# An attention and mixture-of-experts layer whose first stage works in rounded three-part products, with its stores, first score passes, row scatter and last stores rearranged

## The chip, the cores and the metric

The kernel runs on one core of one Trainium2 chip. The metric is the device time of one execution in microseconds (us); "before" is the kernel as it stood, "after" the changed one.

## The reference

One transformer layer on 4096 tokens of width 256. The tokens are normalised, the same `xn` goes through 16-head attention and through a feed-forward part with eight routed experts (two for each token) and one shared expert, and all three are added.

```python
xn = _layernorm(x, axis=-1)                  # x: (1, 4096, 256)
q, k, v = xn @ Wq.T, xn @ Wk.T, xn @ Wv.T    # 16 heads of 16
attn = softmax(einsum('bqhd,bkhd->bhqk', q, k) / sqrt(256))
out  = einsum('bhqk,bkhd->bqhd', attn, v)
scores = softmax(xn @ gate_w.T); idx = top_k(scores + gate_b, 2)
expert(x) = silu((x @ w1 + b1) * (x @ w3 + b3)) @ w2 + b2      # 256 -> 352 -> 256
result = x + out + sum_k scores[idx_k] * expert_idx_k(xn) + shared_expert(xn)
```

## The kernel before

The work is written out by hand for each engine; semaphores order it, and each engine takes its instructions in the order of the code.

**First stage.** The tokens come in eight chunks of 512 (`NCH`). VectorE normalises them (`variances`, `deviations`, `normalise`), TensorE transposes a chunk (`turn_xn`), ScalarE copies it to SBUF (`take_xn`), and `project` makes four blocks (two of queries, two of keys) of 128 rows by 512 tokens, each out of two full-precision matmuls. ScalarE writes a rounded copy of each block (`split`) and its square, VectorE the rest that the rounding left (`residual`), and SyncE stores both to DRAM (`qk_parts`), from where heads are later loaded. `norms` sums the squares; from them a bound on the scores is worked out, which head 0 needs as a shift for each query (`spart`, stored to `qshift_parts`). After the chunks `value_rows` makes the values and the router's inputs in 16 pairs of token tiles, ScalarE copies each pair (`keep_values`), and only then do the scores begin.

**Heads.** A head has 128 groups of scores (`GH`). For each group TensorE does two matmuls of 50 rows (`scores`), ScalarE one exponential of 1024 columns (`probs`), and for each two groups TensorE does four matmuls of values. The semaphore `s_scores` counts groups and is the clock of the other queues. Heads 0 and 15 are plain (`plain_head`). In heads 1 to 14 the feed-forward units are woven in, four for a head (`mixed_head`): unit u does `up_both(u, 0..2)` and the two `down_tile`s of unit u-1, and has 32 groups of scores. Units 0 to 7 are the shared expert on the first tokens (`shared`, `SA = 8`), units 8 to 46 are routed.

**How a unit gets its tokens.** GpSimd loads the tokens of a shared unit from `xnT_rows` (`load_shared`), VectorE splits them in a rounded part and a rest at the end of the unit before (`tokens_hi`, `tokens_lo`), and TensorE waits for this (`s_xboth`) before `up_both(u, 0)`. GpSimd's other work at that time is `scatter`: sixteen times it loads 256 rows of x, normalises them and writes them to their experts' slots with four indirect transfers. Both stand in one queue, in this order:

```python
            scatter(0)
            scatter(1)
            for u in range(SZ + 1):
                if u + 2 < SA or u + 2 in (SZ, SZ + 1):
                    load_shared(u + 2)
                for v in range(2 + 3 * u, min(5 + 3 * u, SH)):
                    scatter(v)
```

So `load_shared(6)` stands behind scatters 0 to 13. The first scatter waits for all 128 groups of head 0. Unit 8 on the SyncE side (`load_slots(8)`) waits for all scatters.

**End.** SyncE stores the last 16 columns of the result when the last head's sum is done.

## Time and profile before

| | us |
|---|---|
| three runs, median (lowest to highest) | 2173.07 (2171.87 to 2174.39) |
| the profiled execution | 2174.21 |
| its span (first to last instruction) | 2172.3 |
| TensorE busy in the span | 2152.4 |
| ScalarE busy | 2009.4 |
| VectorE busy | 800.5 |
| GpSimd busy | 246.0 |

The profiled execution lasted 1.9 us longer than its span. A busy TensorE is not TensorE at its peak: matmuls overlap in the records, so what one costs is read from the distance between starts.

### The profile page before, as it was taken

To read this page: it belongs to the slowest core of one execution; us is meant where nothing else is said; L and a number is where in the kernel's file an instruction comes from. 1 tells how busy PE (TensorE), PEld (TensorE's weight loads), DVE (VectorE), ACT (ScalarE), POOL (GpSimd) and SP (SyncE) were. 2 spreads that over 40 slices of the span, in tenths; PEclk is the share of its full clock that TensorE was granted. 3 is DMA by queue.
4 is the path that set the end of the run, shared out by engine and by line. 5 is a ranking of instruction groups with operands and counts; after the bars stand their busy time and mean duration, and the time that the engine had idled before them with its cause. 6 is when DMAs were issued, how large, how long until landed. Compare 5 with 4: busy or idle time off the path is not lost.

```text
span 2172.3 us, 37982 instructions
## 1 busy us (share of the span) xinstructions
PE 2152.4 (99%) x15638; PEld 965.2 (44%) x15638; DVE 800.5 (37%) x1515; ACT 2009.4 (93%) x2209; POOL 246.0 (11%) x242
## 2 busy tenths in 40 slices
PE   9999999999999999999999999999999999999998
PEld 4632344444444444444444444444444444444322
DVE  6321143344344334334334434334334334544200
ACT  4599999999999999999999999999999999999998
POOL 0100465610000000000000000000000002223200
PEclk9999999999999999999999999999999999999999
DMA  7671334332222222213132222213213222332120
GB/s 254 206 280 33 91 121 130 100 90 66 63 78 63 76 57 79 78 54 85 48 77 70 77 64 69 78 50 83 75 50 90 63 69 75 105 97 66 57 78 3
DMA packets 223595, 187.24 MB, mean 86 GB/s; under 512 B 112039, under 2 KB 194558, under 8 KB 223166
## 3 DMA queue, kind: packets, MB, share of 16 engines
q1 hardware_dynamic: 211598, 149.41, 24.3%
q0 software_dynamic: 11824, 35.40, 5.0%
q8 instruction: 123, 2.02, 0.4%
q14 instruction: 50, 0.41, 0.1%
HBM read 130.21 MB, written 54.53 MB: 85 GB/s over the span
## 4 chain that ended last, share of the span: by engine, by line
PE 92%; ACT 7%; DVE 1%; DMA 0%; issue 0%; DVEq 0%
PE PS L672 41%; PE PS L659 29%; PE PS L684 12%; ACT probs L866 6%; PE PS L695 6%; PE PS L565 2%; PE PS L602 1%; PE PS L575 0%; DVE stats L972 0%; PE PS L554 0%; DMA resid<-in_x 0%; DVE probs L996 0%; ACT probs L818 0%; DVE o_t L1169 0%; DVE mv L975 0%
## 5 line engine op out<-in xcount | busy, mean ns | idle before, releaser
L866 ACT ACTIVATE probs<-PS 128x1024 f32<-128x1024 f32 x2048 | 1920.0, 1080 | 96.0 <-PE PS L659 81.8
L672 PE MATMUL PS<-probs,v_head 128*32 128x512 f32 x8192 | 1002.8, 601 | 1.1 <-ACT probs L866 0.8
L659 PE MATMUL PS<-q_ring,k_stack 50*128 50x512 f32 x4096 | 741.3, 446 | 7.0 <-ACT probs L866 6.2
L659 PEld LDWEIGHTS PS<-q_ring,k_stack 50*128 50x128 f32 x4096 | 332.6, 185 | 627.2 <-ACT probs L866 569.6
L672 PEld LDWEIGHTS PS<-probs,v_head 128*32 128x32 f32 x8192 | 206.6, 108 | 448.2 <-issue 359.6
L1194 DVE TENSOR_SCALAR gate_in<-PS,bias_sb 128x256 f32<-128x256 f32 x165 | 79.6, 482 | 754.9 <-PE PS L684 739.5
L684 PE MATMUL PS<-x_hi,w_hi 128*128 128x256 f32 (+1 forms) x660 | 201.3, 305 | 0.0
L684 PE MATMUL PS<-x_hi,w_lo 128*128 128x256 f32 (+1 forms) x660 | 186.5, 283 | 0.0
L684 PE MATMUL PS<-x_lo,w_hi 128*128 128x256 f32 (+1 forms) x660 | 185.6, 281 | 0.0
L921 POOL DMA_DIRECT2D slot_y<-y_sb x39 | 27.9, 716 | 1285.1 <-DVE y_sb L1262 1251.6
L684 PEld LDWEIGHTS PS<-x_hi,w_hi 128*128 128x128 f32 (+1 forms) x660 | 118.6, 180 | 60.0 <-issue 60.0
L684 PEld LDWEIGHTS PS<-x_lo,w_hi 128*128 128x128 f32 (+1 forms) x660 | 118.5, 180 | 0.0
L684 PEld LDWEIGHTS PS<-x_hi,w_lo 128*128 128x128 f32 (+1 forms) x660 | 118.4, 179 | 0.0
L695 PE MATMUL PS<-w_hi,hid_hi 128*128 128x256 f32 x330 | 99.0, 300 | 0.0
L1262 DVE COPY y_sb<-PS 128x512 f32<-128x512 f32 x39 | 27.0, 692 | 188.6 <-PE PS L695 188.6
L695 PE MATMUL PS<-w_lo,hid_hi 128*128 128x256 f32 x330 | 93.3, 283 | 0.0
L695 PE MATMUL PS<-w_hi,hid_lo 128*128 128x256 f32 x330 | 93.1, 282 | 0.0
L1223 DVE TENSOR_TENSOR w_lo<-w_raw,w_hi 128x1408 fp32r<-128x1408 f32 x55 | 89.7, 1630 | 1.9
L1199 DVE SCALAR_TENSOR_TENSOR prod<-PS,bias_sb,gate_in 128x256 f32<-128x256 f32 x165 | 79.7, 483 | 5.9
L1169 DVE STREAM_TRANSPOSE o_t<-PS 128x512 f32<-128x512 f32 x32 | 22.9, 717 | 154.3 <-PE PS L672 154.2
L914 POOL DMA_INDIRECT slot_x<-y_sb,pos x64 | 70.2, 1097 | 19.1 <-issue 14.3
L695 PEld LDWEIGHTS PS<-w_hi,hid_hi 128*128 128x128 f32 x330 | 62.8, 190 | 13.3 <-issue 13.3
(137 smaller groups left out, 1098.2 us busy)
## 6 DMA issues: line engine op xcount, KB each, us to landing
w_raw<-in_w SPq DMA_DIRECT2D x110, 352.0 KB
k_stack<-qk_parts SPq DMA_DIRECT2D x120, 128.0 KB
w_raw<-in_w SPq DMA_DIRECT2D x55, 256.0 KB
q_ring<-qk_parts SPq DMA_DIRECT2D x384, 32.0 KB
slot_x<-part_a SPq DMA_DIRECT2D x39, 256.0 KB, 2.3
slot_in<-slot_x SPq DMA_DIRECT2D x156, 64.0 KB, 2.4
slot_y<-y_sb POOLq DMA_DIRECT2D x39, 256.0 KB, 2.5
k_stack<-qk_parts SPq DMA_DIRECT2D x136, 64.0 KB
```

The costliest lines, as they stand in the source:

```text
L565: last = pe.matmul(bank(2 + j), wqk[:, j // DT, dt, (j % DT) * P:(j % DT + 1) * P], cols, start=(dt == 0), stop=(dt == DT - 1))
L659: last = pe.matmul(bank(2 * score_buffer(turn, g) + r), k_stack[rows, kt * P:(kt + 1) * P], q_ring[rows, sweep, i * QC:(i + 1) * QC], star ...
L672: last = pe.matmul(bank(O_BANK)[VW * j:VW * (j + 1), :], v_head[:, kt, :], probs[:, slot, (j % 2) * QC:(j % 2 + 1) * QC], start=(kt == 0), ...
L684: last = pe.matmul(f_half(w)[0:FT[j], :], a[u % 2][:, w, dt, j * P:j * P + FT[j]], b[:, dt * CH:(dt + 1) * CH], start=(n == 0), stop=(n == ...
L695: last = pe.matmul(f_half(t), a[0:rows, j, t * P:(t + 1) * P], b[0:rows, j, :], start=(n == 0), stop=(n == 8))
L866: nc.scalar.activation(probs[:, prob_slot(g), :], bank(2 * score_buffer(h, g), 2), ACT.Exp, scale=ENERGY_SCALE).then_inc(s_exp, 1)
L914: nc.gpsimd.indirect_dma_start(out=slot_x, out_offset=bass.IndirectOffsetOnAxis(ap=pos[:, u * TPU + t, k:k + 1], axis=0), in_=rows[:, t, : ...
L921: nc.gpsimd.dma_start(slot_y[(u - SA) * CH:(u - SA + 1) * CH, :].rearrange("(t p) d -> p t d", p=P), y_sb[:, u % 2, :].rearrange("p (t d) ...
L1194: V.tensor_scalar(gate_in[0:FT[j], :], f_half(0)[0:FT[j], :], bias_sb[0:FT[j], u % 2, j:j + 1], 0.5, ALU.add, ALU.mult).then_inc(s_gin, 1)
L1199: V.scalar_tensor_tensor(prod[u % 2][0:FT[j], j, :], f_half(1)[0:FT[j], :], bias_sb[0:FT[j], u % 2, 3 + j:4 + j], gate_in[0:FT[j], :], ALU ...
L1223: V.tensor_tensor(w13_lo[u % 2][:, :, :, :], w13_raw[:, :, :, :], w13_hi[u % 2][:, :, :, :].bitcast(f32), ALU.subtract).then_inc(s_w13, 1)
L1262: V.tensor_copy(y_sb[:, u % 2, :], bank(F_BANK)).then_inc(s_yc, 1)
```

## The change

1. **Rounded products.** Chunk 0 is projected as before. For chunks 1 to 7 and all values, tokens and weights are each split in a rounded part and a rest, and each product becomes three rounded matmuls (high by high, low by high, high by low). ScalarE writes two copies of each transposed chunk (`take_tokens`), VectorE makes the rests (`tokens_low`, and once for the weights).
2. **A new order.** Queries are made with the keys for chunks 0 to 3 only; those of chunks 4 to 7 follow after all keys (`late_queries`). The values of pairs 0 to 9 are made between the projections, pairs 10 to 15 at the end. Stores of keys and queries are separate, and each chunk of tokens is stored to `xnT_rows` as it is made, where before all 4 MB went out in one transfer after the first stage.
3. **Buffers.** Query chunks 6 and 7 are kept in what later are probability buffers and in `part_a`. So `keep_values(12)` waits until the store of query chunk 6 has landed, and group 6 of head 0 waits for the shift's second half.
4. **Shift in halves.** The first half, which head 0's first sweep reads, is stored and loaded before the second is there.
5. **Filler.** Between the first score groups of head 0 TensorE repeats a score matmul pair seven times into banks that nobody reads; the first values come one step earlier. The routing counts stand 4 steps later in head 0.
6. **Scatter.** `scatter(u)` waits for group GH + 32 + 8u, where it was GH + 10u.
7. **Last stores.** Two of the last four stores are issued by ScalarE.

```diff
+FIRST = NCH // 2
+XRING = 4
+PAIRS = NT // 2
+SIDE_PAIR = 5
+LATE_PAIR = 10
+LN_GROUPS = ((0, 4), (4, 8), (8, 12), (12, 16), (16, 24), (24, NT))
+LN_LOAD = (0, 1, 2, 2, 3, 4)
 
...
+def key_job(c):
+
+    return 4 * c if c < FIRST else 4 * FIRST + DT * (c - FIRST)
+
+
+def query_job(c):
+
+    return 4 * c + DT if c < FIRST else 4 * FIRST + DT * c
+
...
+            def store_keys(c):
+
+                for s, ready in enumerate((s_hi, s_res)):
+                    sp.wait_ge(ready, key_job(c) + DT)
+                    sp.dma_start(store_v[s][:, DT:2 * DT, c * QC:(c + 1) * QC], key_part[c % 2][:, s, :, :].bitcast(f32)).then_inc(s_kst[c % 2], 16)
...
+                sp.wait_ge(s_xt, DT * (c + 1))
+                sp.dma_start(x_rows[:, :, c * QC:(c + 1) * QC], xfull[:, c % 2, :, :]).then_inc(s_xd[c % 2], 16)
+                store_keys(c)
                 if c:
-                    sp.wait_ge(s_store[part_of(c - 1)], stored(c - 1))
+                    sp.wait_ge(s_kst[(c - 1) % 2], stored(c - 1))
                     load_k_chunk(c - 1)
-                if c == QCH:
-                    load_q_rows(0, 0)
-            sp.wait_ge(s_store[part_of(NCH - 1)], stored(NCH - 1))
+                if c < FIRST:
+                    store_queries(c)
+            for half in range(2):
+                sp.wait_ge(s_qst[half], stored(FIRST - 2 + half))
+            load_q_rows(0, 0)
+            store_queries(4)
+            store_queries(5)
+            sp.wait_ge(s_kst[(NCH - 1) % 2], stored(NCH - 1))
             load_k_chunk(NCH - 1)
-            for s in range(NP_):
-                sp.wait_ge(s_s1, s + 1)
-                sp.dma_start(qshift_parts[s].rearrange("h (c t) -> c h t", c=NCH), spart[:, s, :].bitcast(f32)).then_inc(s_sst, 16)
+            store_shift(0)
+            store_queries(6)
+            store_queries(7)
+            sp.wait_ge(s_sst, 16 * NP_)
...
+            def project(c, w, i, b):
+
+                cols = slice(i * P, (i + 1) * P)
+
+                def moving(buf, dt):
+                    return buf[:, dt, :] if w else buf[:, dt, :].rearrange("p (t j r) -> p j t r", t=TPC, j=QCH)
+
+                hi, lo = xh[c % XRING], xl[c % XRING]
+                for dt in range(DT):
+                    pe.wait_ge(s_xh, DT * c + dt + 1)
+                    pe.matmul(bank(b), wqk_hi[:, w, dt, cols], moving(hi, dt), start=(dt == 0), stop=False)
+                    pe.matmul(bank(b), wqk_lo[:, w, dt, cols], moving(hi, dt), start=False, stop=False)
+                pe.wait_ge(s_xl, c + 1)
+                for dt in range(DT):
+                    last = pe.matmul(bank(b), wqk_hi[:, w, dt, cols], moving(lo, dt), start=False, stop=(dt == DT - 1))
+                last.then_inc(s_qk, 1)
...
+            def value_rows(n):
+
+                if n == 0:
+                    pe.wait_ge(s_vwl, 1)
+                if n < SIDE_PAIR or n == LATE_PAIR:
+                    pe.wait_ge(s_xt, DT * turned[0])
+                    pe.wait_ge(s_xh, DT * turned[0])
+                if n == SIDE_PAIR:
+                    pe.wait_ge(s_res, query_job(FIRST - 1) + DT)
+                if n == LATE_PAIR + 1:
+                    pe.wait_ge(s_res, NCH * NJ)
+                if n == LATE_PAIR + 2:
+                    pe.wait_ge(s_qn, 2)
+                if 0 < n <= LATE_PAIR:
+                    pe.wait_ge(s_vc, n)
+                if n >= LATE_PAIR + 3:
+                    pe.wait_ge(s_vc, n - 2)
+                for i in range(2):
+                    c, t = (2 * n + i) // TPC, (2 * n + i) % TPC
+                    rows = slice(t * P, (t + 1) * P)
                     for dt in range(DT):
+                        dst = bank(pair_bank(n) + i)[:, 0:VE]
+                        pe.matmul(dst, xh[c % XRING][:, dt, rows], wvg_hi[:, dt, :], start=(dt == 0), stop=False)
+                        pe.matmul(dst, xh[c % XRING][:, dt, rows], wvg_lo[:, dt, :], start=False, stop=False)
+                        last = pe.matmul(dst, xl[c % XRING][:, dt, rows], wvg_hi[:, dt, :], start=False, stop=(dt == DT - 1))
+                last.then_inc(s_v, 1)
+                paired[0] = n + 1
 
...
             turn_first()
+            first_project(1, 0)
+            first_project(1, 1)
+            turn_xn(1)
+            first_project(0, 0)
+            first_project(0, 1)
             pe.wait_ge(s_hb, 2)
-            for c in range(NCH):
-                pe.wait_ge(s_xt, c + 1)
-                project(c, 0)
-                project(c, 1)
+            key_norms(0)
+            for c in range(1, FIRST):
+                keys(c, 0)
+                query_norms(c - 1)
+                keys(c, 1)
+                if c > 1:
+                    value_rows(2 * c - 3)
+                queries(c, 0)
+                turn_xn(c + 1)
+                queries(c, 1)
+                key_norms(c)
+                value_rows(2 * c - 2)
+            for c in range(FIRST, NCH):
+                keys(c, 0)
+                if c == FIRST:
+                    query_norms(FIRST - 1)
                 if c < NCH - 1:
                     turn_xn(c + 1)
-                if c:
-                    norms(c - 1)
-                project(c, 2)
-                project(c, 3)
-            norms(NCH - 1)
-
...
+            late_queries(4, 0)
+            late_queries(4, 1)
             pe.wait_ge(s_mk, 1)
             pe.transpose(bank(7)[0:1, 0:P], kmax[:, 0:1], ident_sb[:, :]).then_inc(s_kt, 1)
-            value_rows(1)
+            late_queries(5, 0)
+            query_norms(4)
+            late_queries(5, 1)
             pe.wait_ge(s_krow, 1)
             pe.matmul(bank(7)[:, P:P + 1], krow[0:1, 0:P], ones_sb[0:1, 0:1], start=True, stop=True).then_inc(s_kb, 1)
-            value_rows(2)
-            value_rows(3)
-            value_rows(4)
+            late_queries(6, 0)
+            query_norms(5)
+            late_queries(6, 1)
+            late_queries(7, 0)
+            query_norms(6)
+            late_queries(7, 1)
+            value_rows(10)
+            query_norms(7)
+            value_rows(11)
             pe.wait_ge(s_gcol, 1)
             pe.transpose(bank(6)[0:1, 0:P], qbound[:, 1:2], ident_sb[:, :]).then_inc(s_grow, 1)
-            for n in range(5, NT // 2):
+            for n in range(12, PAIRS):
                 value_rows(n)
...
+                    if h == 0 and k == 1:
+                        continue
                     next_scores(2)
-                    if h == 0 and k == 20:
+                    if h == 0 and k == 24:
...
+            def filler(count):
+
+                for n in range(count):
+                    for r in range(2):
+                        rows = slice(r * HALF, r * HALF + ROWS)
+                        pe.matmul(bank(F_BANK + r), k_stack[rows, 0:P], q_ring[rows, 0, 0:QC], start=True, stop=True)
+
             next_scores(SB)
+            filler(3)
+            next_scores(1)
+            filler(2)
+            next_scores(1)
+            filler(2)
+            next_values(1)
             plain_head(0)
...
+            def take_tokens(c):
 
                 act.wait_ge(s_tr, c + 1)
...
+            def keep_values(n):
+
+                if n == 12:
+                    act.wait_ge(s_qst[0], stored(6))
+                act.wait_ge(s_v, n + 1)
+                src = bank(pair_bank(n), 2).rearrange("p (i n) -> p i n", i=2)
+                nc.scalar.activation(v_all[:, 2 * n:2 * n + 2, :], src[:, :, 0:VE], ACT.Copy).then_inc(s_vc, 1)
 
...
+                    if h == 0 and g == 6:
+                        act.wait_ge(s_sst, 32 * NP_)
...
+            act.wait_ge(s_resid, SH + SWEEPS)
+            for c in range(NCH - 2, NCH):
+                nc.scalar.dma_start(out_v[:, c * TPC:(c + 1) * TPC, D - HD:D], resid[:, c * TPC:(c + 1) * TPC, D - HD:D]).then_inc(s_out, 16)
...
-                pool.wait_ge(s_scores, GH + 10 * u)
+                pool.wait_ge(s_scores, GH + 32 + 8 * u)
...
+            def tokens_low(c):
+
+                for dt in range(DT):
+                    dve.wait_ge(s_xt, DT * c + dt + 1)
+                    dve.wait_ge(s_xh, DT * c + dt + 1)
+                    last = V.tensor_tensor(xl[c % XRING][:, dt, :], xfull[:, c % 2, dt, :], xh[c % XRING][:, dt, :].bitcast(f32), ALU.subtract)
+                last.then_inc(s_xl, 1)```

TensorE's order in the middle of the first stage, of before: chunk 3 and what follows it (`early` holds the transposed tokens, `hones_b` sums the squares).

```order
L554 MATMUL PS<-ident_sb,probs 128x128 x8
L575 MATMUL PS<-probs,hones_b 128x512 x4
L565 MATMUL PS<-early,probs 128x512 x8
L554 MATMUL PS<-ident_sb,probs 128x128 x8
L575 MATMUL PS<-probs,hones_b 128x512 x4
```

The changed kernel on the same engine, in the chunks that make keys only (`x_parts` holds the two parts of the tokens):

```order
L696 MATMUL PS<-probs,hones_b 128x512 x2
L664 MATMUL PS<-x_parts,wqk_hi 128x512
L665 MATMUL PS<-x_parts,wqk_lo 128x512
L664 MATMUL PS<-x_parts,wqk_hi 128x512
L665 MATMUL PS<-x_parts,wqk_lo 128x512
L668 MATMUL PS<-x_parts,wqk_hi 128x512 x2
L640 MATMUL PS<-ident_sb,probs 128x128 x8
```

Two full-precision matmuls of a block have become six rounded ones, and a chunk has two blocks here where it had four.

ScalarE at the end of the first stage, before: the last blocks, the root for the shift, the value pairs, then the exponentials.

```order
L818 ACTIVATE probs<-PS 128x512
L836 ACTIVATE probs<-PS 128x512 [waits s_nr]
L843 ACTIVATE v_all<-PS 128x528 [waits s_v,s_store1]
L843 ACTIVATE v_all<-PS 128x528 [waits s_v]
L848 ACTIVATE kmax<-PS 128x1 [waits s_kb]
L843 ACTIVATE v_all<-PS 128x528 [waits s_v] x14
L866 ACT_TABLE_LOAD
```

And in the changed kernel (L1031 is the rounded copy of a query block, L1040 a value pair):

```order
L1031 ACTIVATE part_a<-PS 128x512 [waits s_qk]
L1032 ACTIVATE probs<-PS 128x512
L1040 ACTIVATE v_all<-PS 128x528 [waits s_v]
L1092 ACTIVATE probs<-PS 64x512 [waits s_nq]
L1040 ACTIVATE v_all<-PS 128x528 [waits s_v]
L1040 ACTIVATE v_all<-PS 128x528 [waits s_v,s_qst0]
L1040 ACTIVATE v_all<-PS 128x528 [waits s_v] x3
L1112 ACT_TABLE_LOAD
```

The query blocks now stand right before the last value pairs, and pair 12 waits for a store (`s_qst0`).

SyncE's queue ahead of the first scores, in the changed kernel, from the stores of query chunk 5 to the load of the shift:

```order
L455 DMA qk_parts<-part_q 128x2x512 [waits s_hi]
L455 DMA qk_parts<-part_q 128x2x512 [waits s_res]
L414 DMA k_stack<-qk_parts 32x1x512 [waits s_kst1]
L416 DMA k_stack<-qk_parts 16x512
L414 DMA k_stack<-qk_parts 32x1x512
L416 DMA k_stack<-qk_parts 16x512
L463 DMA qshift_parts<-probs 4x16x512 [waits s_s1] x2
L455 DMA qk_parts<-probs 128x2x512 [waits s_hi]
L455 DMA qk_parts<-probs 128x2x512 [waits s_res]
L455 DMA qk_parts<-part_a 128x2x512 [waits s_hi]
L455 DMA qk_parts<-part_a 128x2x512 [waits s_res]
L432 DMA q_ring<-qshift_parts 2x4x128 [waits s_sst]
```

Before, all stores of queries stood ahead of the values; now six of the last eight stand among the loads that the first scores need.

## Rows read from the trace of the kernel before

**Rows 1.** The page: the span.
```profile
span 2172.3 us, 37982 instructions
```

**Rows 2.** Stretches: from:to, length; PE, PEld, DVE, ACT, POOL; clock; DMA; GB/s.
```profile
80.00:90.00 10.00, 8.82 (x38) 6.07 (x37) 5.37 (x11) 4.20 (x9) 6.33 (x3) 1.00 0.96 367
...
1220.00:1260.00 40.00, 40.00 (x310) 18.95 (x300) 14.10 (x24) 38.22 (x42) 0.71 (x1) 1.00 0.27 71
```

**Rows 3.** Chain that ended last, first stage: start us, us, what.
```profile
61.75 6.87 PE PS L565 x16
...
70.35 6.87 PE PS L565 x16
...
93.36 19.60 PE PS L602 x88
```

**Rows 4.** Timeline, first stage, ScalarE and VectorE: start us, us, instruction.
```profile
78.41 0.59 ACT L818 ACTIVATE probs<-PS 128x512 bf16<-128x512 f32 x1
...
78.89 0.60 ACT L817 ACTIVATE part_a<-PS 128x512 fp32r<-128x512 f32 x1
...
23.38 1.28 DVE L1009 TENSOR_TENSOR v_all<-PS,v_all 128x512 fp32r<-128x512 f32 x2
```

**Rows 5.** Timeline of TensorE: rounded products in a unit; chain: two score groups.
```profile
434.59 0.28 PE L684 MATMUL PS<-x_lo,w_hi 128*128 128x256 f32 x1
...
434.71 0.28 PE L684 MATMUL PS<-x_hi,w_lo 128*128 128x256 f32 x1
...
163.29 0.84 PE PS L659 x4
```

**Rows 6.** Timeline and busy time by stretch: the start of head 0.
```profile
113.64 0.96 PE L659 MATMUL PS<-q_ring,k_stack 50*128 50x512 f32 x6 [0.70 <-ACT v_all L843]
...
114.90 4.69 ACT L866 ACTIVATE probs<-PS 128x1024 f32<-128x1024 f32 x5
...
124.55 16.59 ACT L866 ACTIVATE probs<-PS 128x1024 f32<-128x1024 f32 x18
...
116.00:120.00 4.00, 3.59 (x14) 1.14 (x16) 0.00 (x0) 3.58 (x4) 0.00 (x0) 0.57 0.97 414
```

**Rows 7.** Timeline: SyncE's store of a chunk; GpSimd's wait for the last one.
```profile
69.53 3.02 SPq L400 DMA_DIRECT2D qk_parts<-part_a  x2
...
93.39 0.31 POOL L885 MEMSET w_raw<- 32x256 f32 x1 [6.94 <-DMA qk_parts<-part_a]
```

**Rows 8.** Timeline of GpSimd: scatters 0 and 1, loads of units 5, 6.
```profile
234.03 0.72 POOL L904 DMA_DIRECT2D y_sb<-in_x  x1 [111.10 <-PE PS L659]
...
244.86 0.79 POOL L904 DMA_DIRECT2D y_sb<-in_x  x1
...
375.97 0.78 POOL L895 DMA_DIRECT2D slot_in<-xnT_rows  x1
...
416.21 0.79 POOL L895 DMA_DIRECT2D slot_in<-xnT_rows  x1
```

**Rows 9.** Timeline of TensorE and VectorE: scores ahead of up_both(0, 2); starts of units.
```profile
265.88 0.73 PE L659 MATMUL PS<-q_ring,k_stack 50*128 50x512 f32 x4
...
401.33 0.39 PE L684 MATMUL PS<-x_hi,w_hi 128*128 128x256 f32 x1
...
431.26 0.41 DVE L1243 CAST x_hi<-slot_in 128x512 fp32r<-128x512 f32 x1
...
433.64 0.39 PE L684 MATMUL PS<-x_hi,w_hi 128*128 128x256 f32 x1
```

**Rows 10.** Loads of slot_in by GpSimd, 100 to 480 us: time to landing.
```profile
DMA to landing us min/median/max: 2.4/3.0/7.4
```

**Rows 11.** Timeline of TensorE: values after a short wait, and in a steady head.
```profile
256.72 3.49 PE L672 MATMUL PS<-probs,v_head 128*32 128x512 f32 x16
...
640.74 1.92 PE L672 MATMUL PS<-probs,v_head 128*32 128x512 f32 x16
```

**Rows 12.** Timeline of SyncE: the last stores.
```profile
2168.39 2.02 SPq L528 DMA_DIRECT2D out<-resid  x4
```

More of the change, by code:

```diff
@@ L413, in _ @@
+            for half in range(2):
+                sp.wait_ge(s_qst[half], stored(NCH - 2 + half))
             with sp.If(flag):
@@ L493, in next_keys @@
                 load_k_rows(h + 1, i)
+            for half in range(2):
+                sp.wait_ge(s_xd[half], 16 * FIRST)
             load_up(0)
@@ L533, in _ @@
         def _(pe):
+            turned = [0]
+            paired = [0]
             blank = o_t[:, :, :].rearrange("p b d -> p (b d)").bitcast(bf16)
@@ L567, in project @@
                 last.then_inc(s_qk, 1)
-            def norms(c):
-                pe.wait_ge(s_sq, c * NJ + NJ)
-                own = slice(P - H - H * c, 2 * P - H - H * c)
-                for w in range(2):
-                    for dt in range(DT):
-                        last = pe.matmul(bank(6 + w), hones_b[:, dt, own], sq[:, c % 2, w * DT + dt, :],
-                                         start=(c == 0 and dt == 0), stop=(c == NCH - 1 and dt == DT - 1))
-                last.then_inc(s_nr, 1)
@@ new lines, in key_norms, with query_norms @@
+            def key_norms(c):
+                pe.wait_ge(s_sq, key_job(c) + DT)
+                own = slice(P - H - H * c, 2 * P - H - H * c)
+                for dt in range(DT):
+                    last = pe.matmul(bank(7), hones_b[:, dt, own], sq[:, 1, dt, :],
+                                     start=(c == 0 and dt == 0), stop=(c == NCH - 1 and dt == DT - 1))
+                last.then_inc(s_nk, 1)
+            def query_norms(c):
+                pe.wait_ge(s_sq, query_job(c) + DT)
+                own = slice(P - H - H * c, 2 * P - H - H * c)
+                for dt in range(DT):
+                    last = pe.matmul(bank(6 if c < FIRST else 5), hones_b[:, dt, own], sq[:, 0, dt, :],
+                                     start=(c % FIRST == 0 and dt == 0), stop=(c % FIRST == FIRST - 1 and dt == DT - 1))
+                last.then_inc(s_nq, 1)
@@ L845, in _ @@
-            keep_values(0)
-            keep_values(1)
+                keep_values(2 * c - 2)
+            for c in range(FIRST, NCH):
+                split_keys(c, 0)
+                if c < NCH - 1:
+                    take_tokens(c + 1)
+                if c == FIRST:
+                    keep_values(5)
+                split_keys(c, 1)
+                if c == FIRST:
+                    root(5)
+                    act.wait_ge(s_nq, FIRST)
+                    nc.scalar.activation(qnorm[0:HALF, :], bank(6)[0:HALF, :], ACT.Sqrt).then_inc(s_qn, 1)
+                keep_values(c + 2)
@@ L847, in _ @@
+            split_queries(4, 0)
+            split_queries(4, 1)
+            split_queries(5, 0)
+            split_queries(5, 1)
             act.wait_ge(s_kb, 1)
             nc.scalar.activation(kmax[:, 1:2], bank(7)[:, P:P + 1], ACT.Sqrt).then_inc(s_kroot, 1)
-            for n in range(2, NT // 2):
+            split_queries(6, 0)
+            split_queries(6, 1)
+            split_queries(7, 0)
+            split_queries(7, 1)
+            keep_values(10)
+            act.wait_ge(s_nq, NCH)
@@ L850, in _ @@
+            nc.scalar.activation(qnorm[HALF:P, :], bank(5)[HALF:P, :], ACT.Sqrt).then_inc(s_qn, 1)
+            for n in range(11, PAIRS):
                 keep_values(n)
@@ L922, in store_y @@
                                     y_sb[:, u % 2, :].rearrange("p (t d) -> p t d", t=TPU)).then_inc(s_yst[u % 2], 16)
-            pool.wait_ge(s_xd, 16)
+            for half in range(2):
+                pool.wait_ge(s_xd[half], 16 * FIRST)
             load_shared(0)
@@ L1286, in _ @@
             add_output(0)
-            dve.wait_ge(s_xd, 16)
+            for half in range(2):
+                dve.wait_ge(s_xd[half], 16 * FIRST)
             up_hi(0)
```

336 lines of the change are left out of this document (230 added, 106 removed).

## The prediction

> **What bounds the kernel now.** I read the page first for the span [rows 1], then the busy time by stretch. In a mixed head TensorE is busy in all of 40 us and ScalarE in 38.2 [rows 2]: from head 1 to head 14 TensorE sets the pace, with ScalarE close behind, and what makes TensorE wait there comes out whole at the end. Next the chain of waits for the first 114 us. It runs on TensorE nearly throughout: a chunk every 8.60 us (61.75 to 70.35), of which 6.87 are projections, then the values, the last 11 pairs in 19.60 us [rows 3]. The scores start at 113.64 [rows 6], so a microsecond saved ahead of them is one saved at the end, as long as nothing later gives it back. Last the timeline of GpSimd: it has 246 us of work in 2172, but in heads 1 and 2 it works through one queue from 234 to past 416 [rows 8], and units 5, 6 and 7 get their tokens from it. That queue is where this change can lose.
>
> **First stage on TensorE.** A full-precision product of 512 columns is 6.87 / 8 = 0.86 us. A rounded one of 512 columns is 0.84 / 4 = 0.21 where the scores do it with 50 rows; one of 256 columns and 128 rows starts 0.12 after the one before, so twice that, 0.24, is the upper bound [rows 5]. I take 0.215, since the scores have the same number of columns. A block then costs 6 x 0.215 = 1.29 where it cost 1.72. There are 28 blocks in chunks 1 to 7: 12.0 us less (7.8 at 0.24). A value pair costs 19.60 / 11 = 1.78 now; 12 products of 264 columns at 0.124 make 1.49, so 16 pairs give 4.7 us. TensorE's own work falls from about 97.5 to 80.7 us (chunk 0 6.9, the 28 blocks 36.1, transposes 7.0, norms 6.9, values 23.8).
>
> What it waits for grows. ScalarE now does 12 copies for a chunk at 0.48 each, and VectorE two more differences of 0.64 besides its four, all the normalising, and the weights' rest [rows 4]. I walked the orders of the three engines chunk by chunk with these distances. ScalarE keeps up (12 copies and two value pairs, some 6.8 us for a chunk, against 10 on TensorE). VectorE does not: TensorE waits for the normalised chunk 2 (about 2 us), for the low tokens of chunk 2 (1), for chunk 4 (1) and for chunk 6 (2). With the small waits at the start I come to 9 us of idle TensorE where 6 are now, and the last value pair ends near 99.5 where it ends at 112.9.
>
> **SyncE's queue ahead of the scores.** In the changed order, twelve loads of query rows, four stores of query chunks 4 and 5, four loads of key chunk 7, the shift, four stores of chunks 6 and 7 and then the shift's load stand in this order behind the last keys. By my walk the loads begin near 83.5, the stores of chunk 6 near 95.5, the shift's load near 98.5. A pair of 1 MB stores held the queue for 3.02 us when transfers had piled up, and the last chunk's stores (2 MB) landed some 10 us after their issue, with DMA busy 0.96 at 367 GB/s [rows 2, 7]. Query chunks 4 to 7 are 4.2 MB within 12 us, 11.4 us at that rate. So the store of chunk 6 lands near 101, and `keep_values(12)`, with pair 15 and all scores behind it, waits for that; the shift, behind chunk 7, lands near 102.5. I put the first scores at 103 (100 if transfers don't pile up, 107 if each takes the 10 us of the last one). **Term: 113.6 - 103 = 10.6 us saved** (7 to 14).
>
> **Start of head 0.** Now eight exponentials need from 114.90 to 124.55, where the steady 0.92 each makes 7.3; TensorE's granted clock falls to 0.57 of full, that is mostly 1.2 GHz, after two waits of 1.4 and 0.4 us [rows 6]. Seven filler pairs (0.42 each, 0.84 at the low level) cover these waits. If TensorE comes to them from the values, the gain is up to 2 us; if it comes from a wait of 3 us for the store, at 1.2 GHz the fillers stand in the way of groups 3 and 4 and cost up to 2. I expect the second kind of start about as much as the first, and take **0**.
>
> **Last stores.** Four issues hold SyncE for 2.02 us [rows 12]; two queues halve that: **1.0 us saved** (0.5 to 1.2). The Trainium skill says the same of it ("DMA: Bandwidth & Descriptors", "Issuing engines are not separate DMA queues"): a second queue saves only the time to initiate, since both run on the same 16 DMA engines. No row before shows a store from ScalarE.
>
> **Scatter.** Group 160 is scored just before `up_both(0, 2)`, at 266.5; the wait for group 128 ended at 234.0 [rows 8, 9]. So the first scatter starts 32.5 us later in the course of the heads. The waits of the later ones (8 groups, 8.1 us) are shorter than a scatter (some 12.8 us, below), so only the first counts, and everything in the queue moves with it. The load of unit 6 is issued at 416.2, lands 3.0 later [rows 8, 10], and needs 1.2 for its two splits; unit 6 starts at 433.6 [rows 9]. That is 13.2 us of slack, and the shift is 32.5: TensorE waits 19.3 us in all. The same sum for unit 5 (375.97 against 401.33) gives some 11, of which the wait for unit 6 is the continuation, not an addition; unit 7 is no later than unit 6 already made it. Bounds: 14 scatters and 4 loads took 182 us, that is 12.8 for a scatter, and the quickest took 10.8 [rows 8]. At 10.8 for each the load would go out at 266.5 + 151 + 3 = 421 and nobody would wait. The long ones are those whose load of x meets SyncE's loads of queries and keys; moved by one unit they meet them about as often. I placed the 14 among SyncE's transfers and came to 13.5 to 17.4. I take **16 us lost** (11 to 19), nearer the measured row.
>
> When TensorE comes back from such a wait it is at 1.2 GHz: 16 value records took 3.49 us after short waits where 1.92 is usual [rows 11]. The earlier waits' price falls into the last wait; these records alone lost 1.6. With a little more for what stands behind them, the last wait costs **1.9 us** (1.6 to 2.5). The Trainium skill ("TensorE: Matmul & The Clock Gate", "HAM oscillation — how this bites in real kernels") has it that each such wait for a transfer is paid again in clock; by it three waits would cost 3 x 1.9 = 5.7, and the sum would be 3.8 us higher. That speaks against this change, but here the first two are covered.
>
> The rest costs nothing: the routing's counts at step 24 of head 0 are ready by then, `load_slots(8)` waits for the last scatter at a time when TensorE itself has been moved back, and POOL's `memset`s have 20 us of cover.
>
> **Sum.** 2174.2 (the profiled execution) - 10.6 - 0 - 1.0 + 16 + 1.9 = 2180.5. The median of the runs is 1.1 lower, so 2179.4; I say 2179.
>
> **Rivals.**
> A. The scatter costs nothing (18 in 100): with the other engines' traffic elsewhere each takes 11 us or less. For it: the quickest of 10.8. Against it: the 14 took 12.8 on average [rows 8], with the same traffic beside them that they will meet again. Time: 2179.4 - 17.9 = 2161.5, and 2157 to 2166 with the bounds of the first stage. This is the other side, and it decides if the load of unit 6 goes out before 429.4 on the clock of before.
> B. The gains are at their upper and the wait at its lower bound: first scores at 100, fillers give 1.5, wait 12 and 1.9: 2173.1 - 13.6 - 1.5 - 1.0 + 13.9 = 2171. The saving and the loss cancel. With its neighbours, 24 in 100.
> C. The first stage saves little (8 in 100): VectorE or the transfers make TensorE wait more, or the clock falls in the 2 us wait for chunk 2; scores from 107 and the full wait: 2173.1 - 6.6 - 1 + 21.2 = 2187.
> D. The forecast, 50 in 100: 2175 to 2184.
>
> **Numbers.** 0.2% is 4.3 us, about what a measurement of this kernel can tell from no change. Faster (under 2168.8): rival A and the edge of B, 0.23. Same (to 2177.4): most of B and the lower part of D, 0.26. Slower: 0.51. Leaving out a tenth at either end, the range is 2160 to 2187; that of the forecast alone is 2175 to 2184.
>
> **What the profile would show.** First stage: blocks 1.29 us from start to start of their groups, last value pair by 100, first scores at 103 with the wait before them put down to a transfer. Scatter: the first y_sb load as `up_both(0, 2)` begins; TensorE's longest waits before `up_both(4..6, 0)`, put down to VectorE's `tokens_lo` or the load of slot_in, in all 16 us, and the clock at its low level behind them. I am wrong if GpSimd's queue runs at 11 us for a scatter, or if the scores start before 99.

## The result, and the profile after

| | time, us | ratio to before, with its 95% interval |
|---|---|---|
| before, in the same session | 2173.73 (2171.87 to 2174.58) | |
| after | 2192.61 (2191.09 to 2195.18) | 1.0087 [1.0075, 1.0099] |

The change makes the kernel slower by 0.87%, 19 us. The forecast was 2179, with a range up to 2187. The direction was right, the size was not. First where the scores of head 0 begin (timeline of TensorE after):

```profile
117.77 1.65 PE L829 MATMUL PS<-q_ring,k_stack 50*128 50x512 f32 x6 [0.70 <-ACT v_all L1040]
```

They began at 113.64 [rows 6]: the stage that was to save 10.6 us loses 4.1. The busy time by stretch shows that TensorE is idle for almost 9 of the 20 us from 60 to 80, at a granted clock of 0.79 (columns as in [rows 2]):

```profile
60.00:80.00 20.00, 11.27 (x56) 9.15 (x56) 15.06 (x20) 8.09 (x16) 8.22 (x4) 0.79 0.54 178
```

The timelines of TensorE, VectorE and GpSimd after, in that stretch, say why:

```profile
66.23 0.69 DVE L1260 TENSOR_TENSOR x_parts<-x_full,x_parts 128x512 fp32r<-128x512 f32 x1 [0.29 <-ACT x_full L998]
67.21 0.69 DVE L1267 TENSOR_TENSOR part_a<-PS,part_a 128x512 fp32r<-128x512 f32 x1 [0.29 <-ACT probs L1017]
67.82 8.71 DVE L1248 TENSOR_SCALAR probs<-resid,mv,rstd 128x256 f32<-128x256 f32 x4
...
67.90 0.96 POOL L1127 MEMSET v_head<- 128x1024 f32 x1 [66.66 <-PE PS L696]
68.92 7.14 POOL L1130 MEMSET k_stack<- 2x4096 f32 x2
76.11 0.18 POOL L1132 MEMSET v_head<- 128x32 f32 x1
...
76.58 1.75 PE L640 MATMUL PS<-ident_sb,probs 128*128 128x128 f32 x7 [7.36 <-DVE probs L1248]
```

`normalise(7)` takes 8.71 us where the same four take 1.37 without a memset beside them (e3, below), and it ends with GpSimd's memsets. Taken one by one the four last 1.19, 3.68, 3.68 and 0.40 us, beside memsets of 0.96, 3.54, 3.54 and 0.18. TensorE waits 7.36 us for its transposes. Then the end of the stage, ScalarE and SyncE after:

```profile
104.83 0.61 ACT L1040 ACTIVATE v_all<-PS 128x528 f32<-128x528 f32 x1 [0.94 <-PE PS L733]
113.40 1.62 ACT L1040 ACTIVATE v_all<-PS 128x528 f32<-128x528 f32 x3 [7.96 <-DMA qk_parts<-probs]
...
106.05 2.33 SPq L455 DMA_DIRECT2D qk_parts<-probs  x2
108.42 2.93 SPq L455 DMA_DIRECT2D qk_parts<-part_a  x2
111.39 3.30 SPq L432 DMA_DIRECT2D q_ring<-qshift_parts  x4
```

`keep_values(12)` waits 7.96 us for the store of query chunk 6, issued at 106.05. The shift's load ends its issue only at 114.7. Third, heads 1 to 3: GpSimd's first load of y_sb and its load of unit 6, TensorE's waits from 340 to 480 (us in total, times, longest), and a stretch of busy time:

```profile
269.78 0.72 POOL L1155 DMA_DIRECT2D y_sb<-in_x  x1 [150.11 <-PE PS L829]
...
447.86 0.79 POOL L1146 DMA_DIRECT2D slot_in<-xnT_rows  x1
...
PE PS L854 <- DVE x_lo L1561: 13.1, 3, 5.4
...
340.00:490.00 150.00, 136.94 (x1004) 64.56 (x1007) 50.76 (x87) 125.28 (x136) 81.57 (x75) 0.94 0.36 113
```

The load of unit 6 went out at 416.21 [rows 8] and goes out at 447.86. TensorE waits 4.97, 5.36 and 2.73 us for the tokens of units 4, 5 and 6, with a low clock behind each wait (granted clock 0.55 from 416 to 420, 0.72 from 452 to 456). Last the stores at the end, two queues side by side:

```profile
2190.04 0.92 SPq L607 DMA_DIRECT2D out<-resid  x2
```

### The profile page after: what moved, and what is told of

The parts are those of the page before. It is cut to its first block, busy times and chain, and to the rows that moved or that the text cites. A ratio compares the mean times of both kernels' runs of the same rounds, so it can differ in the third digit from the quotient of the medians.

```text
span 2193.4 us, 38378 instructions
## 1 busy us (share of the span) xinstructions
PE 2148.7 (98%) x15765; PEld 982.4 (45%) x15772; DVE 822.1 (37%) x1541; ACT 2019.9 (92%) x2229; POOL 245.8 (11%) x242
## 4 chain that ended last, share of the span: by engine, by line
PE 87%; ACT 7%; DMA 2%; POOL 2%; DVE 1%; issue 1%; SPq 0%; DVEq 0%; POOLq 0%; ACTq 0%
PE PS L842 39%; PE PS L829 28%; PE PS L854 12%; ACT probs L1112 6%; PE PS L865 6%; POOL slot_x L1165 1%; DMA y_sb<-in_x 1%; DVE probs L1248 1%; POOL y_sb L1159 1%; DMA slot_in<-xnT_rows 0%; PE PS L664 0%; PE PS L665 0%; PE PS L668 0%; PE PS L640 0%; DMA qk_parts<-probs 0%
## 5 line engine op out<-in xcount | busy, mean ns | idle before, releaser
L1112 ACT ACTIVATE probs<-PS 128x1024 f32<-128x1024 f32 x2048 | 1920.2, 1080 | 113.2 <-PE PS L829 98.0
L829 PE MATMUL PS<-q_ring,k_stack 50*128 50x512 f32 x4096 | 741.7, 446 | 5.6 <-ACT probs L1112 4.0
L829 PEld LDWEIGHTS PS<-q_ring,k_stack 50*128 50x128 f32 x4096 | 333.1, 185 | 623.9 <-ACT probs L1112 564.6
L854 PE MATMUL PS<-x_hi,w_hi 128*128 128x256 f32 (+1 forms) x660 | 202.6, 307 | 13.1 <-DVE x_lo L1561 13.1
L854 PE MATMUL PS<-x_hi,w_lo 128*128 128x256 f32 (+1 forms) x660 | 187.8, 285 | 0.0
L854 PE MATMUL PS<-x_lo,w_hi 128*128 128x256 f32 (+1 forms) x660 | 186.9, 283 | 0.0
L854 PEld LDWEIGHTS PS<-x_hi,w_hi 128*128 128x128 f32 (+1 forms) x660 | 119.8, 181 | 73.2 <-issue 73.2
L854 PEld LDWEIGHTS PS<-x_lo,w_hi 128*128 128x128 f32 (+1 forms) x660 | 119.9, 182 | 0.0
L854 PEld LDWEIGHTS PS<-x_hi,w_lo 128*128 128x128 f32 (+1 forms) x660 | 119.8, 181 | 0.0
```

What stands on the lines that cost most here:

```text
L829: last = pe.matmul(bank(2 * score_buffer(turn, g) + r), k_stack[rows, kt * P:(kt + 1) * P], q_ring[rows, sweep, i * QC:(i + 1) * QC], star ...
L854: last = pe.matmul(f_half(w)[0:FT[j], :], a[u % 2][:, w, dt, j * P:j * P + FT[j]], b[:, dt * CH:(dt + 1) * CH], start=(n == 0), stop=(n == ...
L1112: nc.scalar.activation(probs[:, prob_slot(g), :], bank(2 * score_buffer(h, g), 2), ACT.Exp, scale=ENERGY_SCALE).then_inc(s_exp, 1)
```

## The experiments

They ran in three sessions, each on a chip of its own, in which the kernel before took 2170.1, 2173.4 and 2172.4 us (medians of 24, 19 and 14 runs). So only ratios to before are compared across sessions; 0.001 is 2.2 us.

| run | ratio to before | first scores, us |
|---|---|---|
| after | 1.0087 [1.0075, 1.0099] | 117.8 |
| e1: scatter back | 1.0015 [1.0005, 1.0024] | 117.8 |
| e2: memsets late | 1.0045 [1.0028, 1.0062] | 109.5 |
| e3: both | 0.9979 [0.9969, 0.9989] | 109.5 |
| e4: before, scatter moved | 1.0065 [1.0048, 1.0082] | 113.5 |
| e5: before, memsets early | 1.0007 [0.9997, 1.0016] | 115.2 |
| e6: e3, own buffer for chunk 6 | 0.9980 [0.9971, 0.9990] | 107.9 |
| e7: e6, shift's load first | 0.9975 [0.9965, 0.9984] | 104.5 |
| e8: after, memsets beside tokens_low | 1.0052 [1.0035, 1.0069] | 110.9 |
| e9: e7, both shift stores first | 0.9961 [0.9947, 0.9975] | 105.0 |
| e10: e9 without fillers | 0.9952 [0.9935, 0.9968] | 103.6 |
| e11: e3, scatter moved by half | 0.9980 [0.9970, 0.9989] | 109.4 |
| e12: e9, last stores from one queue | one run, 2169.3 us | 105.9 |

The first scores are read from one trace each. VectorE's reduction of the last key norms (`kmax`), which no edit of theirs should move, starts at 78.8 to 79.3 us in e2, e3, e6, e7, e9, e10 and e11, and at 80.4 and 80.2 in e8 and e12. So differences of half a microsecond between two starts mean nothing, and e8 and e12 were over a microsecond late before it; in e8 that is so at 59 us already, ahead of the memsets that it moves.

**e1: the scatter back.**

```diff
-                pool.wait_ge(s_scores, GH + 32 + 8 * u)
+                pool.wait_ge(s_scores, GH + 10 * u)
```

> The changed kernel with one part undone: the scatters wait for scores GH + 10u again. Theory (the later start of the scatters makes TensorE wait for the tokens of units 4 to 6): the scores still start at 117.8 us, the first load of y_sb goes out near 237 instead of 269.8, the waits of 5.0, 5.4 and 2.7 us in heads 2 and 3 are gone with the low clock behind them, and the time falls by 16 to 19 us, to 2175 (2172 to 2178). Rival (these waits come from the loads beside them, not from where the scatters start): they stay, and the time is 2188 or more.

The three waits are gone. Against after the ratio falls by 0.0072, 15.6 us (half-width of the two intervals together 3.4). Two outputs of the attention heads, before and behind the waits, show the loss in the traces (VectorE's timeline; after, then e1):

```profile
306.25 0.72 DVE L1483 STREAM_TRANSPOSE o_t<-PS 128x512 f32<-128x512 f32 x1 [1.14 <-PE PS L842]
...
518.22 0.72 DVE L1483 STREAM_TRANSPOSE o_t<-PS 128x512 f32<-128x512 f32 x1 [0.49 <-PE PS L842]
```

```profile
303.13 0.72 DVE L1483 STREAM_TRANSPOSE o_t<-PS 128x512 f32<-128x512 f32 x1 [0.48 <-PE PS L842]
...
497.01 0.72 DVE L1483 STREAM_TRANSPOSE o_t<-PS 128x512 f32<-128x512 f32 x1 [0.49 <-PE PS L842]
```

211.97 us against 193.88: 18.1 lost, of which 13.1 are waits and the other 5.0 what TensorE does more slowly behind them: in e1 the granted clock is 1.00 throughout this stretch, in after it is 0.92 between outputs 3 and 4. The rival falls.

**e2: the memsets late, and e3: both.**

```diff
-            pool.wait_ge(s_nk, NCH - 2)
+            pool.wait_ge(s_nk, NCH)
```

> The changed kernel with GpSimd's memsets of v_head and k_stack held back until all eight key norms are done (s_nk NCH instead of NCH - 2), so that they no longer lie beside normalise(7). Theory (the memsets slow VectorE's copy from SBUF to SBUF): normalise(7) takes 1.4 us instead of 8.7, TensorE's wait of 7.4 us for it and the low clock behind it are gone, the late query blocks come 8 us earlier; the store of query chunk 6 then lands near 105 and the scores start at 109 (106 to 112) instead of 117.8: time 2184 (2181 to 2187). Rival (VectorE is slow there because of the piled-up transfers or because of its own order): normalise(7) still takes over 5 us, and the time stays within 2 us of 2192.6.

> Both edits together: scatters at GH + 10u, memsets after the eighth key norm. If the two losses have nothing to do with each other, the gains add: 2192.6 - 17.9 - 8.6 = 2166 (2162 to 2171), faster than the kernel before by 0.3%. Rival (an earlier start of head 0 makes the routing or the loads late, or the store of chunk 6 holds the scores where they are): 2172 or more, no better than the kernel before.

e2 takes 0.0042 off, 9 us (half-widths together 4.5). In e3 the same edit takes 0.0036 off e1, 8 us (3.0): within these intervals the two losses add. In both, normalise(7) takes 1.37 us again and the clock stays at 1.00; VectorE, then the stretch of e3 that answers to the one of after:

```profile
67.83 1.37 DVE L1248 TENSOR_SCALAR probs<-resid,mv,rstd 128x256 f32<-128x256 f32 x4
...
60.00:80.00 20.00, 18.52 (x105) 14.93 (x104) 11.69 (x25) 12.97 (x25) 1.11 (x2) 1.00 0.72 253
```

The store of chunk 6 holds ScalarE as before (8.87 us), so the scores come 8.3 us earlier (109.46), the middle of what was expected. e3 is 0.2% faster than the kernel before.

**e5: the kernel before with its memsets early** (`s_nr, NCH - 1` becomes `NCH - 3`), so that they meet its own normalise(7).

> The kernel before with one edit: its memsets start after five norms instead of seven, near 60 us instead of 78, so that they lie beside normalise(7) (61 to 63 us). Theory (GpSimd's memsets slow VectorE where it reads and writes SBUF): the four normalising instructions go from 0.41 us each to about 2, TensorE waits 4 to 7 us for them, and the time rises by 4 to 9 us, to 2178 to 2183. Rival (only the new order or its transfers made VectorE slow): they stay at 0.41 each and the time stays at 2173.7 within 2 us.

The collision is there, in a kernel with nothing else changed (VectorE, GpSimd, TensorE of e5):

```profile
61.28 8.65 DVE L996 TENSOR_SCALAR probs<-resid,mv,rstd 128x256 f32<-128x256 f32 x4
...
62.33 7.14 POOL L880 MEMSET k_stack<- 2x4096 f32 x2
...
69.99 1.09 PE L554 MATMUL PS<-ident_sb,probs 128*128 128x128 f32 x8 [1.87 <-DVE probs L996]
```

But it costs 1.9 us on TensorE, not the expected 4 to 7, and 0.0007 of the time, which can't be told from nothing: by the time alone the rival's number came true, and only the trace speaks for the theory. VectorE came 7.3 us late, and over 5 of them lay under blocks that TensorE had ready; in the new order the transposes of chunk 7 come so early that all of it is waiting. The mechanism was right, my price for this kernel wrong, since I counted the whole delay as waiting.

**e8: which VectorE instructions does a memset hold?**

```diff
             pool.wait_ge(s_nk, NCH - 2)
+            pool.wait_ge(s_xn, NCH - 1)
```

> The changed kernel with GpSimd's memsets held back only until normalise(7) is done (s_xn NCH - 1 as well), so that they lie from 70 to 78 us beside tokens_low(7), two TENSOR_TENSOR whose sources and target are all in SBUF, and beside differences that read PSUM. Theory (the memset blocks only VectorE's one-source operations from SBUF to SBUF): normalise(7) takes 1.4 us, tokens_low keeps its 0.69 for each, and the time is that of the run with late memsets, 2192.6 - 9 to 10, a ratio of 1.0045 to before. Rival (whatever VectorE does within SBUF is blocked): the first tokens_low takes 5 to 7 us, TensorE waits for it, and 4 us or more of the gain are lost, a ratio over 1.006.

The memsets now lie from 70.92 to 79.26. VectorE and GpSimd of e8:

```profile
73.11 0.69 DVE L1261 TENSOR_TENSOR x_parts<-x_full,x_parts 128x512 fp32r<-128x512 f32 x1 [0.35 <-ACT x_full L998]
74.08 0.69 DVE L1261 TENSOR_TENSOR x_parts<-x_full,x_parts 128x512 fp32r<-128x512 f32 x1 [0.29 <-ACT x_full L998]
75.06 0.69 DVE L1268 TENSOR_TENSOR part_a<-PS,part_a 128x512 fp32r<-128x512 f32 x1 [0.29 <-ACT probs L1017]
...
71.95 7.09 POOL L1131 MEMSET k_stack<- 2x4096 f32 x2
```

Two sources in SBUF: 0.69 each, as without a memset. One source in PSUM: 0.69. Of these only the one-source TENSOR_SCALAR within SBUF is held. The time (1.0052) is that of e2 within the intervals.

Two more records draw the line finer. In e3 the late memsets are not free either: they meet a COPY of one row within SBUF. VectorE of e3, then the same COPY in after, where no memset lies beside it:

```profile
82.31 1.13 DVE L1331 COPY krow<-krow 1x128 f32<-1x128 f32 x1
```

```profile
91.53 0.22 DVE L1331 COPY krow<-krow 1x128 f32<-1x128 f32 x1
```

In e3 it ends at 83.44, just behind the first memset of `k_stack` (from 79.84, 3.52 us). All eight runs with memsets this late (e2, e3, e6, e7, e9 to e12) show 1.12 or 1.13 for it. And in the kernel before, a one-source reduction within SBUF lay wholly under a memset and kept its time, the 0.69 us that it takes in e5 with no memset beside it:

```profile
84.40 0.69 DVE L1036 TENSOR_REDUCE qbound<-probs 128x1 f32<-128x512 f32 x1
```

So the theory of e8, that every one-source instruction within SBUF is blocked, was too wide: TENSOR_SCALAR and COPY were held, TENSOR_REDUCE was not.

**e4: the kernel before with the scatter moved** (`GH + 10 * u` becomes `GH + 32 + 8 * u`).

> The kernel before with one edit: the scatters wait for scores GH + 32 + 8u. Theory (the later start is a loss of its own, whatever the first stage does): TensorE waits before up_both of units 4, 5 and 6 as in the changed kernel, 13 us in all with the low clock behind it, and the time rises by 15 to 19 us, a ratio near 1.008 to before. Rival (in the kernel before, with the scores 4 us earlier, the slack of units 5 and 6 takes most of the shift): 8 us or less, a ratio under 1.004.

0.0065, 14 us: the loss belongs to the scatter alone. The waits in its trace are three again, 11.5 us in all, the longest 6.1 (13 in all expected). The time is a microsecond under the low end of what I expected, far from the rival's 8.

**e11: half the shift, on e3** (`GH + 16 + 9 * u`).

> The kernel with both parts undone (e3), but the scatters wait for scores GH + 16 + 9u: half the shift. Theory (only the first scatter's start counts, and unit 6 has 13.2 us of slack): the first load of y_sb 16.3 us later, TensorE waits 3 us in all (2 to 5) before unit 5 or 6, with 1.7 to 3.4 of clock behind: 4 to 8 us more than e3, a ratio of 1.000 to 1.0015 to before. Rival (the loss is in proportion to the shift, since every scatter meets worse traffic): half of the 15.6 us, that is 8 or more, a ratio over 1.0015, and the 14 scatters take longer than in e3.

The first load of y_sb went out at 244.43 instead of 227.84, the load of unit 6 at 421.65 instead of 407.36. TensorE waits for no token, and the ratio is that of e3. So the loss isn't in proportion to the shift; it is what goes beyond the slack. The 3 us of waiting that I expected did not come: the queue was 2.3 us quicker between the two loads (177.2 against 179.5), and the heads themselves stood 3 us later by then (output 4 at 427.19 against 424.04).

**e6, e7, e9: what holds the scores when the memsets don't.** In e6 query chunk 6 gets a part of x_parts that is free by then; in e7 the shift's load goes ahead of the two last stores; in e9 the second shift store too.

```diff
-        query_part = [..., in_stage, in_xn, key_part[0]]
+        in_ring = x_parts[:, 0:NP_ * DT * QC].rearrange(...)
+        query_part = [..., in_stage, in_ring, key_part[0]]
...
-                    act.wait_ge(s_qst[0], stored(6))
+                    act.wait_ge(s_qst[0], stored(4))
...
             store_shift(0)
-            store_queries(6)
-            store_queries(7)
             sp.wait_ge(s_sst, 16 * NP_)
             load_q_shift(0, 0, s_q[0])
+            store_shift(1)      # e9 alone
+            store_queries(6)
+            store_queries(7)
```

> The kernel with both parts undone (e3), and query chunk 6 put into the part of x_parts that is free by then, with a semaphore of its own, so that keep_values(12) waits only for the store of chunk 4. Theory (the scores are held twice, by this store and then by the load of the shift, which SyncE issues only from 103 to 106): ScalarE's wait of 8.9 us is gone, the last value pair ends near 101, but the scores wait for the shift until 107, so that only 2 us (0 to 3) come back against e3: 2170.1 - 5 - 2, a ratio of 0.997 to before. Rival (the store is the only thing that holds them): scores from 102, 6 to 8 us less than e3, a ratio under 0.995.

> As the run with a buffer of its own for chunk 6 (e6), and SyncE issues the load of the shift ahead of the stores of chunks 6 and 7 instead of behind them. Theory (order in SyncE's queue is what is left): the shift's load is issued from about 99 to 102, the scores start at 103 to 105 instead of 109, 5 us (4 to 7) less than e3, a ratio of 0.9955 to before. Rival (TensorE's or ScalarE's own work, or the loads of the query rows, end later than that): less than 3 us against e3.

> As the run with the shift's load ahead of the stores (e7), and SyncE issues also the second shift store ahead of the stores of chunks 6 and 7. Theory (of the 5 us that the scores came earlier there, 2 were given back because the seventh exponential waited for this store, and 1.7 because a wait in head 1 there ended at 1.2 GHz): that wait of 1.8 us is gone, output 0 is taken 2 us earlier than in e7, near 167, and the time is 1 to 2 us less, a ratio of 0.9970 to before (0.996 to 0.998). Rival (what is won ahead of head 0 is always given back in head 1): output 0 earlier, output 2 again at 294.6, and the time as in e7.

The starts came as expected. TensorE's first scores in e3, e6 and e7:

```profile
109.46 0.97 PE L829 MATMUL PS<-q_ring,k_stack 50*128 50x512 f32 x6 [0.70 <-ACT v_all L1040]
```

```profile
107.90 1.65 PE L831 MATMUL PS<-q_ring,k_stack 50*128 50x512 f32 x6 [5.64 <-issue]
```

```profile
104.47 1.54 PE L831 MATMUL PS<-q_ring,k_stack 50*128 50x512 f32 x6 [2.56 <-issue]
```

The chunk's buffer is worth 1.6 us of start, the order in SyncE's queue 3.4, each good to half a microsecond. The wait that the profile can't name ("issue") begins with the end of the last value pair and ends 1.8 us (e6) and 1.4 us (e7) after SyncE has issued the shift's load; that it is this load rests on the order of the edits and is not shown by the trace itself. But the times hardly follow: e6 is as e3, e7 is 0.0004 under it where 0.0024 were expected. Output 0 of e7 is taken 2.9 us earlier than in e3 (169.02 against 171.92), output 2 only 0.2 (294.61 against 294.78). Of the 5 us, 2 went because the seventh exponential waited 1.8 us for the second shift store. The rest went in head 1, where e7's trace has the low clock behind short waits that e3's has not (last section: 16 value records in 3.61 us against 1.92), so that part need not belong to the edit. In e9 the wait for the shift store was gone, and the gain with it: TensorE was now mostly at 1.2 GHz from 104 to 112 (granted clock 0.58 and 0.57) and came late itself (ScalarE waits 1.72 us for it at 112.45), output 0 at 169.89, output 2 at 295.07. Neither side foresaw this: both had output 0 earlier than in e7, and it came 0.9 us later. The ratio is under that of e7, at the low end of what I expected, but the intervals overlap, so whether e9 is any faster than e7 stays open.

**e10: without the fillers.**

> As e9 without the seven filler pairs at the start of head 0. Theory (they cover waits for ScalarE, and at 1.2 GHz they stand in the way of the next scores about as much): the start of head 0 within 1 us of e9, TensorE at 1.2 GHz for some us more, time the same within 2 us. Rival (without them the clock stays low and the start takes 2 to 4 us more): output 0 taken 2 us or more later.

From the first scores to output 0 it takes 65.2 us (103.64 to 168.83), with fillers 64.9 (105.03 to 169.89). They are worth 0.3 us here, as far as two traces tell, and here is a start at the low clock with or without them (granted clock 0.69 and 0.50 from 104 to 112 in e10, 0.58 and 0.57 in e9); what they do for a start like e3's (0.88 from 108 to 112, then 1.00) no run tests. Against e3 the scores start 5.8 us earlier. How much of that reached the end stays open: 0.0027 by the ratios (half-widths together 0.0019), that is 5.9 us, but 2.4 at output 2 by the traces (292.41 against 294.78). This kernel, 0.5% faster than the one before and 1.3% than the changed one, is the best that I found, though its interval overlaps that of e9.

**e12: the last stores from one queue**, on e9; one run, read in its trace.

> As e9 with the last four stores from SyncE alone, as in the kernel before. Theory: from the last addition to resid to the span's end 0.5 us more than with two queues (3.9 against 3.4), nothing else changes; far below what the times can tell, so the trace decides. Rival: no difference, since the two last stores share the DMA engines and their landing takes the time.

```profile
2163.71 2.02 SPq L609 DMA_DIRECT2D out<-resid  x4
```

From this issue to the span's end it is 3.8 us (2167.5), in e9 3.3 (2161.19 to 2164.5). The other traces agree: 3.3 to 3.4 us in all ten with two queues, 3.8 to 3.9 in all four with one (before, e4, e5, e12). Two queues save half a microsecond, and the rival falls. The run's time, 4 us above e9's median, says nothing of the stores: 3.2 us of it are there by output 5 (492.90 against 489.71).

## Why the prediction missed

**The step that failed** is the sentence at the end of the part on costs, "POOL's memsets have 20 us of cover". I asked only who needs what they write. They needed no cover; they took VectorE away: GpSimd starts them at the sixth key norm, which in the new order comes just ahead of normalise(7). By e2 and e3 that is 8.3 us of first scores and 8 to 9 us of time. Without it the time would have lain inside my range: with the memsets late (e2) the ratio of 1.0045 makes 2183.5 of 2173.7. The profile of before had the memsets at 78 us, beside VectorE's differences and reductions, which kept their time, and one COPY that took 0.06 longer than in e5, so it showed no harm. The Trainium skill ("SBUF — State Buffer", "Who interferes with whom") has this as a lock: a TENSOR_SCALAR or copy within SBUF that uses both of VectorE's ports and any GpSimd instruction exclude each other, while one with two SBUF inputs is held only by a GpSimd instruction that reads. The first half agrees with e5 (four TENSOR_SCALAR in 8.65 us instead of 1.37). The second agrees with e8, where the memset reads nothing and the two-input differences kept 0.69. By its rule and the order of before and after the loss could have been forecast: three of four instructions that wait for memsets of 0.96, 3.54 and 3.54 us.

**First scores at 103.** They came at 117.8. The runs tell what each wait held: memsets 8.3 (e3), the wait for the store of chunk 6 another 1.6 (e6), the order of SyncE's queue 3.4 (e7). The last two were in my forecast as waits, too small by 6.5 us together (109.5 in e3 against 103): a mis-sized term. I had named the right last wait, the store of chunk 6, with the shift close behind, but put their landing at 101 and 102.5. Even without the memsets (e3) the store was issued at 97.65, where I had 95.5, and freed ScalarE at 105.1; the shift's load was issued from 103.1 to 106.4, where I had 98.5, since the stores ahead of it held the queue 2.2 to 3.0 us a pair. That is 4.1 of the 6.5; the other 2.4 lie between the store and the scores, where the last four copies and value pair 15 took 4.4 us and I had 2. TensorE's part was nearly right: without the memsets and the wait for the store (e6, e7, e9, e10) the last value pair ends at 102 where I said 99.5. A rounded block costs 1.49 (e10: 81.49 to 82.98, products 0.233 apart), not 1.29; I chose 0.215 by the row of the scores, and the dearer bound of 0.24 was nearer. A value pair costs 1.46 where I had 1.49. Of rival C, that VectorE makes TensorE wait and the clock falls behind it, the mechanism came true; I gave it 8 in 100 and priced it at 4 us.

**Scatter.** 17.9 us forecast; 14.1 (e4), 14.3 (e2 against e3) and 15.6 (e1) by the times, each within some 4 us, and 18.1 by the traces of after and e1. The rule, shift less slack, was right, and e11 shows that half the shift is free. Its two parts were off in opposite ways: 13.1 of waiting for 16, 5.0 behind the waits for 1.9. The Trainium skill's rule that each wait for a transfer is paid again in clock ("TensorE: Matmul & The Clock Gate", "HAM oscillation — how this bites in real kernels") made it 5.7, and the trace is with the rule: I had taken the first two as covered. Behind the waits of 4.97 and 2.73 us the next value records took 2.87 and 2.35 instead of 1.92; behind that of 5.36 the products of `up_both` stood 0.21 us apart instead of 0.12. Rival A is dead in all four kernels that have this scatter (after, e2, e4, e8).

**Start of head 0.** 0 forecast. From the first scores to output 0 (VectorE's first STREAM_TRANSPOSE of o_t) it takes 64.5 us before (113.64 to 178.10) and 63.3 after (117.77 to 181.10): 1.1 saved, within the 2 that I allowed either way. In e1, e2 and e3, with the same fillers, it takes 62.5. **Last stores.** 1.0 forecast, 0.5 measured.

**Sum.** By the outputs of before and after: 4.1 lost at the first scores, 1.1 saved by output 0, 0.2 lost by output 2, 17.4 from there to output 5 (303.10 to 497.68 before, 306.25 to 518.22 after), 1.1 between outputs 28 and 29, for which I have no cause (the clock is 0.97 there in both), and 0.5 saved at the end. 2174.2 + 4.1 - 1.1 + 0.2 + 17.4 + 1.1 - 0.5 = 2195.4, against 2195.2 for the profiled execution.

## What to carry to other kernels

When a reordering lets an idle engine start its work earlier, ask not only who needs the result but whom the work disturbs while it runs: a memset on GpSimd belongs beside VectorE instructions that read PSUM or, as in e8, two tiles of SBUF. A queue of transfers is not its last wait; take one away, and here the next stood less than two microseconds behind it, so look for the whole list (buffer, order, load) before pricing the first. And a start moved forward by 5 us is worth what is left at a point some heads later: 0.2 us at output 2 in e7 and 2.4 in e10, so look there, and in more than one trace.

## What the hardware did that I had not expected

A memset over 2 partitions by 4096 columns takes 3.54 us on GpSimd, 0.86 ns a column, where one over 128 partitions by 1024 takes 0.96, 0.94 ns a column. So by these two shapes the columns set the time, and a memset over two rows holds VectorE for all of it; no run has 128 rows by 4096 columns. VectorE gets one instruction in between two of them: the four of normalise(7) after start at 67.8, 68.9, 72.5 and 76.1 us.

The granted clock behind the same short waits is not always the same. After and e3 have the same three waits of 0.64, 0.41 and 0.42 us in head 1. TensorE after, then e3:

```profile
256.89 0.51 PE L829 MATMUL PS<-q_ring,k_stack 50*128 50x512 f32 x2 [0.64 <-ACT probs L1112]
257.81 0.50 PE L829 MATMUL PS<-q_ring,k_stack 50*128 50x512 f32 x2 [0.41 <-ACT probs L1112]
258.73 0.50 PE L829 MATMUL PS<-q_ring,k_stack 50*128 50x512 f32 x2 [0.42 <-ACT probs L1112]
259.16 3.60 PE L842 MATMUL PS<-probs,v_head 128*32 128x512 f32 x16
```

```profile
247.71 0.51 PE L829 MATMUL PS<-q_ring,k_stack 50*128 50x512 f32 x2 [0.64 <-ACT probs L1112]
248.63 0.50 PE L829 MATMUL PS<-q_ring,k_stack 50*128 50x512 f32 x2 [0.41 <-ACT probs L1112]
249.54 0.50 PE L829 MATMUL PS<-q_ring,k_stack 50*128 50x512 f32 x2 [0.42 <-ACT probs L1112]
249.97 1.92 PE L842 MATMUL PS<-probs,v_head 128*32 128x512 f32 x16
```

3.60 against 1.92. From output 1 to output 2 the traces of e1, e2 and e3 show 64.3 us, those of e6, e10 and e11 65.0 to 65.7, and the other eight, before and after among them, 65.9 to 67.0. The granted clock of this stretch is 1.00 in the traces of e1, e2, e3, e6 and e10 and 0.97 in all others. I found nothing in the instructions that tells them apart; what decides it stays open. It is large enough to hide changes of one or two microseconds in a single trace.
